# Graph kernel, two layers: source indices loaded first, and the first eight row gathers issued ahead of the branch on edge order

## Chip, cores, metric
One core of a Trainium2 chip. The metric is the device time of one execution in microseconds (us); the kernel before takes 2122.07 us, the median of three runs (2119.05, 2122.07 and 2122.08).

## What is computed
There are 6250 nodes with 128 features and 106250 edges (831 tiles of 128 edges, the last one partly filled), sorted by target node `dst` in the inputs given.

```
h = relu(layernorm(x));  x = x + segment_sum((h @ W.T + b)[src] * edge_weight, dst)        # layer 0
h = relu(layernorm(x));  m = relu([h[src], h[dst]] @ W1[t] + b1[t]) @ W2[t] + b2[t]        # layer 1, t = edge type
gi = segment_sum(m, dst) @ W_ih.T + b_ih;  gh = h @ W_hh.T + b_hh;  x = x + GRU(gi, gh, h)
```

## The kernel before
Every engine runs a straight list of instructions; semaphores tie the lists together. All engines first run a prologue, then `choose`: it waits for a flag that VectorE computes from `dst` and `edge_weight` (`dve_scan`, `dve_flag`: are the targets in an order the fast path can take, and no weight negative), loads the flag into a register and branches. With the inputs given the fast branch is taken: `f0_*` for layer 0, `f1_*` for layer 1. The other branch (`l0_*`, `l1_*`, with `sp_x`) is never run here.

In the prologue the SyncE queue loads the four edge arrays whole, 104 partitions of 1024 edges, in the order `dst`, `src`, `edge_weight`, `edge_type` (`load_edges`, three DMAs each; the second waits for a memset of VectorE, `dve_pads`). Each array is then turned so that a tile's 128 edges lie down the partitions. For `src` that is: ScalarE makes floats (L457, `act_float`), TensorE transposes eight blocks (L545, `pe_edges`), ScalarE copies them to `src_t` (L473, `act_edges`), which raises the semaphore `preC` to 1.

GpSimd issues all gathers: one indirect DMA fetches the 128 source rows (512 B each) of one tile. In layer 0 eight tiles make an octet; `f0_pool` (L1297) goes over 104 octets with a ring of `R0` = 6 buffers (`slot0`), so an octet waits for TensorE to have used the one six octets earlier (`out0`). Octets 0 to 6 gather rows of the input `x`, which are normalised after they come in (`edge_stats`, `weigh_early`). From octet 7 (`EARLY`) on the rows come from `h0_tab`, a table of normalised rows that is made meanwhile: SyncE loads `x` (L381), VectorE takes statistics, ScalarE normalises (L1469), SyncE stores (L1609), and GpSimd waits for the stores (`tab`). Ten tiles of layer 0 are fetched row by row by SyncE instead (L1647), so GpSimd issues 821 gathers. Layer 1 (`f1_pool`, L1673) starts when all of `p_tab` is stored and issues 824 more, in groups of four with a ring of ten.

VectorE's work after the flag: L634 to L644 are seven passes over 104x1024 elements (`dve_rel`, `dve_keys`), then the branch and layer 0's masks (L1312 to L1314).

Of the kernel before, what the change touches and what calls it, by code (L numbers as in the profile page):

```python
# [32 lines left out]
GT = 4  # L33
PR = 2
GP = GT // PR
NG = 4
# [8 lines left out]
def gnn_program(nc, x, src, dst, etype, eweight, W0, b0, W1, b1, W2, b2, Wih, Whh, bih, bhh, out):  # L45
    N, D = x.shape
# [4 lines left out]
    NTILE = -(-E // P)  # L51
# [3 lines left out]
    PB = NT // PR // NBLK  # L55
# [10 lines left out]
    h0_tab = nc.dram_tensor("h0_tab", [N, D], F32).ap()  # L66
# [10 lines left out]
    with ExitStack() as ctx:  # L77
        def sb(name, shape, dt=F32):
            return ctx.enter_context(nc.sbuf_tensor(name, shape, dt))
# [16 lines left out]
        dst_i, src_i, typ_i = tmp(0, I32), tmp(1, I32), tmp(2, I32)  # L96
# [6 lines left out]
        src_t = sb("src_t", [P, NCOL], I32)  # L103
# [32 lines left out]
        rowno = sb("rowno", [P, 2, UT], I32)  # L136
# [46 lines left out]
        R0, R1 = 6, 10  # L183
        FW = D + T + 1
        HR = 4
        TO = NBLK * PR
        NPAIR = NCH // 2
        NOCT = NT // (NBLK * PR)
# [6 lines left out]
        def slot0(k):  # L195
            return accs[:, F0 + k * TO * FW:F0 + (k + 1) * TO * FW].rearrange("p (t f) -> p t f", f=FW)
# [11 lines left out]
        EARLY = 7  # L208
# [5 lines left out]
        alone0, alone1 = ({k: j for j, (k, _) in enumerate(a)} for a in (ALONE0, ALONE1))  # L214
# [80 lines left out]
        s_g0 = [[sem(f"s_gather0_{q}_{h}") for h in range(2)] for q in range(R0)]  # L295
# [45 lines left out]
        LR = 96  # L341
# [11 lines left out]
        def load_edges(eng, ap, to, pads, ev):  # L353
            flat = to.rearrange("p g e -> p (g e)")
            eng.dma_start(flat[0:LR, :], ap[0:LR * OCT].rearrange("(p e) -> p e", e=OCT)).then_inc(s[ev], 16)
            eng.wait_ge(s["pads"], pads)
            eng.dma_start(flat[LR:n_full, :], ap[LR * OCT:n_full * OCT].rearrange("(p e) -> p e", e=OCT)).then_inc(s[ev], 16)
            eng.dma_start(flat[n_full:PB, 0:n_tail], ap[E - n_tail:E].rearrange("(a e) -> a e", a=1)).then_inc(s[ev], 16)
# [7 lines left out]
        W12_IN = 4 * 16  # L366

        def sp_prologue(eng):
            load_edges(eng, dst, dst_i, 1, "dst_in")
            load_edges(eng, src, src_i, 2, "src_in")  # L370
            load_edges(eng, eweight, w_a, 4, "w_in")
            load_edges(eng, etype, typ_i, 3, "typ_in")
            eng.wait_ge(s["qpad"], 1)
            eng.dma_start(q_tab[N:NPAD, :], zrows[0:NPAD - N, :]).then_inc(s["st_q"], 16)
            for k in ("st_c", "st_h", "st_p", "upd_st"):
                eng.sem_inc(s[k], 16)
# [34 lines left out]
            return v  # L411

        def sp_x(eng):
            for i, (a, b) in enumerate(PIECES):
                for h in HALVES:
                    eng.dma_start(x_rows[h, a:b, :], x_lin[h, a:b, :]).then_inc(s_x[i], 16)
            eng.wait_ge(s["xs_pad"], 1)
            for a, b in PIECES:
                for h in HALVES:
                    eng.dma_start(xs[h, a:b, 0:D], x_mod[h, a:b, :]).then_inc(s["x_again"], 16)  # L420
# [144 lines left out]
        def pool_sums(eng):  # L565
            eng.memset(xs[:, :, :], 0.0).then_inc(s["xs_pad"], 1)
# [6 lines left out]
            eng.wait_ge(s["step"], in_order[0])  # L573

        def dve_pads(eng):
            eng.memset(dst_i[LR:PB, :, :], int(FAR)).then_inc(s["pads"], 1)
            eng.memset(src_i[LR:PB, :, :], 0).then_inc(s["pads"], 1)
            eng.memset(typ_i[LR:PB, :, :], 0).then_inc(s["pads"], 1)
            eng.memset(w_a[LR:PB, :, :], 0.0).then_inc(s["pads"], 1)

# [260 lines left out]
        def l0_pool(eng):  # L841
            def sweep_end(w):

                eng.wait_ge(s["out0"], (w + 1) * (NB * NG) + RING)
                apart(eng)
                for k in (q[0] for q in s_g0[:NG]):
                    eng.dma_reset(range(k.num, k.num + 1))
                    eng.sem_clear(k)
                eng.sem_inc(s["swept0"], 1)

            h0_stored(eng)
            eng.memset(accs[:, 0:A0], 0.0).then_inc(s["zero"], 1)

            def step(j, n, q, w, left):
                g = Group(j, n, q)
                eng.wait_ge(s["idx0"], g.gi + 1)
                apart(eng)
                for t in range(GT):
                    k = g.slot * GT + t
                    eng.indirect_dma_start(G[:, g.slot, t, :], None, h0_tab,  # L860
                                           bass.IndirectOffsetOnAxis(rowno[:, 0, k:k + 1], 0)).then_inc(s_g0[g.slot][0], 16)
            layer(eng, step, lambda c, pairs, k: None, sweep_end=sweep_end)

        def l0_dve(eng):
# [95 lines left out]
        def l0_pe(eng):  # L960
            eng.sem_inc(s["out0"], RING)
            MP.start(eng)
            eng.wait_ge(s["preC"], 6)
            eng.wait_ge(s["sets"], 1)
            eng.wait_ge(s["w12_in"], W12_IN)

            def step(j, n, q, w, left):
                g = Group(j, n, q)
                eng.wait_ge(*grp("hot0", g))
                eng.wait_ge(s_g0[g.slot][0], g.gathered)  # L970
                pairs_in(eng, "acc0", g, back=1)
                o = pb[g.two]
                for t in range(GT):
                    p = t // PR
                    eng.matmul(o[:, p * WIN:(p + 1) * WIN], G[:, g.slot, t, :], nodew[:, g.slot, t, :],
                               start=t % PR == 0, stop=t % PR == PR - 1)
                for t in range(GT):
                    p = t // PR
                    ins = eng.matmul(o[0:T + 1, 256 + p * WIN:256 + (p + 1) * WIN], typew[:, g.slot, t, :],
                                     nodehot[:, g.slot, t, :], start=t % PR == 0, stop=t % PR == PR - 1)  # L980
                ins.then_inc(s["out0"], 1)

            def sweep_end(w):
                eng.wait_ge(s["swept0"], w + 1)

            def chunk(c, pairs, k):
                if k == 0:
                    MA.wait(eng, "cnt", c)
                    MD.wait(eng, "x1", c, 1)
                    MP.done(eng.transpose(pb[6][0:CW, 0:D], st[:, 0, 0:CW], ident[:, :]))  # L990
                if k == 2:
                    MD.wait(eng, "h", c)
                    MA.wait(eng, "hT", c, 1)
                    MP.done(eng.transpose(pb[6][:, 256:256 + CW], st[0:CW, 0, P:2 * P], ident[0:CW, 0:CW]))
                if k == 3:
                    MA.wait(eng, "hT", c)
                    MA.wait(eng, "p", c, 1)
                    MP.done(eng.matmul(pb[7][0:CW, :], h1s[:, :], w1a[:, :, :].rearrange("f t g -> f (t g)"),
                                       start=True, stop=True))
                    MD.wait(eng, "q", c, 1)  # L1000
                    MP.done(eng.matmul(pb[5][0:CW, :], h1s[:, :], w1b[:, :, :].rearrange("f t g -> f (t g)"),
                                       start=True, stop=True))
            layer(eng, step, chunk, sweep_end=sweep_end)
# [278 lines left out]
        def pair_at(o, after):  # L1282
            c, r = divmod(o - after - 2 * (LAG + 1), 4)
            return c if r == 0 and 0 <= c < NPAIR else None

        def f0_pool(eng):
            eng.wait_ge(s["preC"], 1)
            for o in range(NOCT):
                if o >= R0:
                    eng.wait_ge(s["out0"], o - R0 + 1)  # L1290
                if o == EARLY:
                    eng.wait_ge(s["tab"], 32 * len(T_PIECES))
                for t in range(TO):
                    k = o * TO + t
                    if k in alone0 or k >= NTILE:
                        continue
                    eng.indirect_dma_start(slot0(o % R0)[:, t, 0:D], None, x if o < EARLY else h0_tab,  # L1297
                                           bass.IndirectOffsetOnAxis(src_t[:, k:k + 1], 0)).then_inc(s_g0[o % R0][t // GT], 16)

        def f0_dve(eng):  # L1300
            eng.wait_ge(s["preC"], 4)
# [628 lines left out]
        def choose(eng, fast, general):  # L1930

            eng.wait_ge(s["prep"], 1)
            ordered = nc.values_load(flag_i[0:1, 0:1], engines=[eng.engine], min_val=0, max_val=1)
            before = in_order[0]
            with eng.If(ordered):
                for f in fast:
                    f(eng)
            in_order[0] = before
            with eng.Else():
                for f in general:  # L1940
                    f(eng)
# [44 lines left out]
        @block.gpsimd  # L1986
        def _(eng):
            pool_prologue(eng)
            pool_sums(eng)
            choose(eng, [f0_pool, f1_pool], [pool_h0, l0_pool, l1_pool])  # L1990

# [18 lines left out]
```

## Time and profile before
| | |
|---|---|
| profiled execution: time, span | 2122.12 us, 2120.3 us |
| runs | 2119.05, 2122.07, 2122.08 us |
| GpSimd (POOL) busy | 1565.8 us, 74% |
| TensorE, VectorE, ScalarE busy | 1265.0, 900.6, 571.0 us |
| DMA | 214.40 MB, mean 101 GB/s |

Span is first to last instruction of the profiled execution; its time is 1.8 us longer. GpSimd's busy share looks moderate, but it counts only the gathers themselves and not the issue gap ahead of each; the waits and the chain of work tell whether it ever stands idle for another engine.

### The profile page before, as it was taken

What the parts mean: (1) busy time and instruction counts of PE and PEld (TensorE: products, weight loads), DVE (VectorE), ACT (ScalarE), POOL (GpSimd) and SP (SyncE); (2) the same over time, 40 slices, a digit from 0 to 9 for tenths busy, and PEclk for the clock granted to TensorE, in tenths of its full rate; (3) what the DMA queues carried; (4) which work ended last, traced back from release to release, by engine and by line L of the source; (5) the groups of instructions that cost most, each with busy time, mean ns of one, the idle gap of its engine ahead of it and who ended that gap; (6) DMA issues with size and microseconds to landing.
All of it is one profiled execution on the core that took longest, in us unless ns stands there. A gap on an engine that the chain in (4) does not pass through costs nothing.

```text
span 2120.3 us, 29576 instructions
## 1 busy us (share of the span) xinstructions
PE 1265.0 (60%) x6646; PEld 1082.7 (51%) x6646; DVE 900.6 (42%) x2542; ACT 571.0 (27%) x1502; POOL 1565.8 (74%) x1658
## 2 busy tenths in 40 slices
PE   2445445445445445445556777776677667677776
PEld 2433333334334334334345676666666666666665
DVE  7633232332332333233234555555555455555454
ACT  4633333333333333333231111111111111111111
POOL 6777777777777777777567777777777777777774
PEclk7566667666666666666668877888988887888887
DMA  8323323333333333323244444444444444444442
GB/s 190 95 81 89 90 78 93 87 80 90 87 81 90 89 80 91 88 80 94 67 132 110 109 109 115 116 109 111 118 110 114 115 110 116 114 111 114 114 114 61
DMA packets 179672, 214.40 MB, mean 101 GB/s; under 512 B 55311, under 2 KB 125585, under 8 KB 178992
## 3 DMA queue, kind: packets, MB, share of 16 engines
q0 software_dynamic: 52640, 107.91, 21.0%
q1 hardware_dynamic: 125608, 103.77, 16.9%
q10 hardware_dynamic: 1244, 0.79, 0.2%
q8 instruction: 56, 0.92, 0.2%
q14 instruction: 124, 1.02, 0.2%
HBM read 176.31 MB, written 35.99 MB: 100 GB/s over the span
## 4 chain that ended last, share of the span: by engine, by line
POOL 73%; issue 24%; PE 1%; DMA 1%; DVE 1%; ACT 0%; POOLq 0%; SPq 0%; DVEq 0%; ACTq 0%
POOL accs L1297 36%; POOL G L1673 15%; POOL edge L1673 15%; POOL g_more L1673 7%; DMA accs<-in_edge_weight_dram 0%; PE bank L1580 0%; DMA accs<-h_tab,src_t 0%; PE bank L1543 0%; PE bank L1883 0%; DMA p_tab<-hot 0%; DMA edge<-p_tab,src_t 0%; ACT accs L1458 0%; PE bank L1896 0%; PE bank L1906 0%; PE bank L1907 0%
## 5 line engine op out<-in xcount | busy, mean ns | idle before, releaser
L1297 POOL DMA_INDIRECT accs<-h_tab,src_t x765 | 722.2, 944 | 233.2 <-issue 232.6
L1872 PE MATMUL bank<-qwin,hotT 128*128 128x128 f32 x1662 | 300.1, 336 | 307.7 <-DVE hotT L1760 296.9
L1543 PE MATMUL bank<-accs 128*125 128x133 f32 x1662 | 329.3, 369 | 220.8 <-ACT accs L1458 172.5
L1543 PEld LDWEIGHTS bank<-accs 128*125 128x125 f32 x1662 | 308.5, 272 | 263.4 <-issue 127.8
L1872 PEld LDWEIGHTS bank<-qwin,hotT 128*128 128x128 f32 x1662 | 255.3, 235 | 343.0 <-DVE hotT L1760 329.5
L1673 POOL DMA_INDIRECT G<-p_tab,src_t x334 | 316.1, 946 | 122.2 <-issue 101.5
L1673 POOL DMA_INDIRECT edge<-p_tab,src_t x331 | 313.8, 948 | 100.9 <-issue 100.6
L1458 ACT ACTIVATE accs<-accs,edge 128x128 f32<-128x128 f32 x765 | 244.4, 391 | 478.9 <-DMA accs<-h_tab,src_t 478.8
L1830 ACT ACTIVATE rows<-rows 128x512 f32<-128x512 f32 x208 | 130.9, 630 | 654.5 <-DVE rows L1770 637.1
L1883 PE MATMUL bank<-hot,rows 128*128 128x128 f32 x1662 | 284.8, 329 | 1.9 <-ACT rows L1830 1.1
L1883 PEld LDWEIGHTS bank<-hot,rows 128*128 128x128 f32 x1662 | 269.2, 246 | 2.3 <-ACT rows L1830 2.3
L1312 DVE COPY accs<-edge 128x8 f32<-128x8 f32 x104 | 20.1, 193 | 474.7 <-PE bank L1543 474.4
L1673 POOL DMA_INDIRECT g_more<-p_tab,src_t x159 | 151.8, 955 | 48.5 <-issue 48.5
L1580 PE MATMUL bank<-w1a,h1b 128*125 128x512 f32 x100 | 93.2, 1086 | 123.1 <-ACT h1b L1492 123.1
L1755 DVE TENSOR_TENSOR hot<-bank,key_t 128x512 f32<-128x512 f32 x208 | 141.6, 681 | 3.6 <-DMA q_tab<-hot 3.6
L1770 DVE TENSOR_TENSOR rows<-bank,G 128x512 f32<-128x512 f32 (+1 forms) x84 | 57.8, 689 | 192.5 <-DMA G<-p_tab,src_t 187.2
L1770 DVE TENSOR_TENSOR rows<-bank,edge 128x512 f32<-128x512 f32 (+1 forms) x84 | 57.4, 684 | 184.1 <-DMA edge<-p_tab,src_t 178.0
L1808 DVE TENSOR_TENSOR accs<-bank,accs 128x128 f32 x416 | 119.5, 287 | 30.6 <-DVE accs L1808 0.7
L1314 DVE TENSOR_TENSOR accs<-bank,edge 128x1000 f32<-128x1000 f32 x104 | 123.8, 1190 | 0.0
L1580 PEld LDWEIGHTS bank<-w1a,h1b 128*125 128x125 f32 x100 | 28.9, 320 | 156.4 <-ACT h1b L1492 125.0
L1558 PE MATMUL bank<-w0t,G 128*125 128x128 f32 x100 | 29.9, 452 | 120.6 <-ACT G L1476 120.6
L1896 PE MATMUL bank<-accs,w 128*128 128x125 f32 x400 | 97.9, 401 | 0.6 <-ACT st L1843 0.6
(178 smaller groups left out, 1322.1 us busy)
## 6 DMA issues: line engine op xcount, KB each, us to landing
qwin<-q_tab SPq DMA_DIRECT2D x416, 64.0 KB
hotT<-h_tab SPq DMA_DIRECT2D x1162, 0.5 KB
nodew<-key_tab SPq DMA_DIRECT2D x52, 256.0 KB
nodehot<-key_tab SPq DMA_DIRECT2D x52, 256.0 KB
w1a<-p_tab SPq DMA_DIRECT2D x778, 0.5 KB
accs<-h_tab,src_t POOLq DMA_INDIRECT x765, 2.5
p_tab<-st SPq DMA_DIRECT2D x25, 224.0 KB
p_tab<-hot SPq DMA_DIRECT2D x25, 224.0 KB
```

Source lines behind the costliest of these rows:

```text
L1297: eng.indirect_dma_start(slot0(o % R0)[:, t, 0:D], None, x if o < EARLY else h0_tab, bass.IndirectOffsetOnAxis(src_t[:, k:k + 1], 0)).then ...
L1314: eng.tensor_tensor(ones_of(o % HR), mid(iota_p[:, 0:CW], TO), bcast(rel_t[:, cols], CW), ALU.is_equal).then_inc(s["hot0"], 1)
L1458: ins = eng.activation(G0[:, t, 0:D], row, ACT.Copy, scale=w_t[:, o * TO + t:o * TO + t + 1])
L1543: ins = eng.matmul(pb[SUM_BANK[o % 4]][0:CW, 0:FW], ones_of(o % HR)[:, t, :], slot0(o % R0)[:, t, :], start=t == 0, stop=t == last)
L1580: ins = eng.matmul(pb[PQ_BANK[k]][0:CW, :], h1_pair[:, k * CW:(k + 1) * CW], weights[:, :, :].rearrange("f t g -> f (t g)"), start=True, s ...
L1673: eng.indirect_dma_start(slot1(g % R1)[:, t, :], None, p_rows, bass.IndirectOffsetOnAxis(src4_t[:, k:k + 1], 0)).then_inc(s_g1[g % R1], 16)
L1755: eng.tensor_tensor(hot[:, g % NG], mid(iota_p, GT), bcast(key_t[:, g * GT:(g + 1) * GT], KEYS), ALU.is_equal)
L1770: ins = eng.tensor_tensor(rows[:, g % 2, 0:n], got[:, 0:n], slot1(g % R1)[:, 0:n], ALU.add)
L1808: eng.tensor_tensor(a, pb[4 + g % 2][:, p * KEYS:(p + 1) * KEYS], a, ALU.add).then_inc(s["acc1"], 1)
L1830: eng.activation(rows[:, g % 2], rows[:, g % 2], ACT.Relu).then_inc(s["relu1"], 1)
L1872: ins = eng.matmul(pb[2 + g % 2][:, t * D:(t + 1) * D], hotT[:, g % HT, t * P:(t + 1) * P], qwin[:, g % NG, t // PR, :], start=True, stop= ...
L1883: ins = eng.matmul(pb[4 + g % 2][:, p * KEYS:(p + 1) * KEYS], rows[:, g % 2, t, :], hot[:, g % NG, t, :], start=t % PR == 0, stop=t % PR = ...
```

## The change
The load order becomes `src`, `dst`, `edge_weight`, `edge_type`, and VectorE's first two memsets swap with it. The body of the gather loop becomes `octet_rows`; `pool_first_octet`, which waits for `preC` and issues octet 0's eight gathers from `x`, runs on GpSimd ahead of `choose`. `f0_pool` starts at octet 1. The other lines (`sp_x`, the shift of `s_g0` by one slot) belong to the branch that isn't run: there the eight gathers have to be waited for and their semaphores kept apart.

```
         def sp_prologue(eng):
-            load_edges(eng, dst, dst_i, 1, "dst_in")
-            load_edges(eng, src, src_i, 2, "src_in")
+            load_edges(eng, src, src_i, 1, "src_in")
+            load_edges(eng, dst, dst_i, 2, "dst_in")
...
         def dve_pads(eng):
+            eng.memset(src_i[LR:PB, :, :], 0).then_inc(s["pads"], 1)
             eng.memset(dst_i[LR:PB, :, :], int(FAR)).then_inc(s["pads"], 1)
-            eng.memset(src_i[LR:PB, :, :], 0).then_inc(s["pads"], 1)
...
+        def octet_rows(eng, o, table):
+            for t in range(TO):
+                k = o * TO + t
+                if k in alone0 or k >= NTILE:
+                    continue
+                eng.indirect_dma_start(slot0(o % R0)[:, t, 0:D], None, table,
+                                       bass.IndirectOffsetOnAxis(src_t[:, k:k + 1], 0)).then_inc(s_g0[o % R0][t // GT], 16)
+
+        def pool_first_octet(eng):
+            eng.wait_ge(s["preC"], 1)
+            octet_rows(eng, 0, x)
+
         def f0_pool(eng):
-            eng.wait_ge(s["preC"], 1)
-            for o in range(NOCT):
+            for o in range(1, NOCT):
                 if o >= R0:
                     eng.wait_ge(s["out0"], o - R0 + 1)
                 if o == EARLY:
                     eng.wait_ge(s["tab"], 32 * len(T_PIECES))
...
+                octet_rows(eng, o, x if o < EARLY else h0_tab)
...
             pool_sums(eng)
+            pool_first_octet(eng)
             choose(eng, [f0_pool, f1_pool], [pool_h0, l0_pool, l1_pool])
```

GpSimd's instructions from its last memset of the prologue (`xs`) on, before: the load of the flag and the branch, then all layer 0 gathers.

```order
L566 MEMSET xs 128x6783
L1933 TENSOR_LOAD flag_i
L1933 ISA x2
L1935 COMPARE_AND_BRANCH
L1297 DMA accs<-in_x_dram,src_t 128x128 x56
L1297 DMA accs<-h_tab,src_t 128x128 x765
```

The same place on GpSimd after the change:

```order
L568 MEMSET xs 128x6783
L1293 DMA accs<-in_x_dram,src_t 128x128 x8
L1941 TENSOR_LOAD flag_i
L1941 ISA x2
L1943 COMPARE_AND_BRANCH
L1293 DMA accs<-in_x_dram,src_t 128x128 x48
L1293 DMA accs<-h_tab,src_t 128x128 x765
```

Eight of the 56 gathers from `x` now stand ahead of the load of the flag; the number of gathers is the same.

The SyncE queue's first DMAs of the program, before (`accs` holds all four edge arrays at this stage):

```order
L355 DMA accs<-in_dst_dram 96x1024
L357 DMA accs<-in_dst_dram 7x1024
L358 DMA accs<-in_dst_dram 1x778
L355 DMA accs<-in_src_dram 96x1024
L357 DMA accs<-in_src_dram 7x1024
L358 DMA accs<-in_src_dram 1x778
```

and after:

```order
L355 DMA accs<-in_src_dram 96x1024
L357 DMA accs<-in_src_dram 7x1024
L358 DMA accs<-in_src_dram 1x778
L355 DMA accs<-in_dst_dram 96x1024
L357 DMA accs<-in_dst_dram 7x1024
L358 DMA accs<-in_dst_dram 1x778
```

Two loads of the same size change places; the weights and types behind them keep theirs.

## Rows read from the trace of the kernel before
**Rows 1.** The page's chain of work that ended last.
```profile
POOL 73%; issue 24%; PE 1%; DMA 1%; DVE 1%; ACT 0%; POOLq 0%; SPq 0%; DVEq 0%; ACTq 0%
```
**Rows 2.** Waits of GpSimd: waited for: us in total, times, longest us.
```profile
POOL accs L1297 <- issue: 260.5, 819, 11.1
POOL G L1673 <- DMA p_tab<-hot: 20.6, 1, 20.6
POOL accs L1297 <- PE bank L1543: 0.6, 2, 0.3
```
**Rows 3.** Timeline of GpSimd's gathers: start, us, instruction, [idle before <-releaser].
```profile
19.08 1.14 POOL L1297 DMA_INDIRECT accs<-in_x_dram,src_t  x1 [11.11 <-issue]
20.53 1.52 POOL L1297 DMA_INDIRECT accs<-in_x_dram,src_t  x1 [0.30 <-issue]
...
23.61 0.94 POOL L1297 DMA_INDIRECT accs<-in_x_dram,src_t  x1 [0.30 <-issue]
24.86 1.98 POOL L1297 DMA_INDIRECT accs<-in_x_dram,src_t  x1 [0.31 <-issue]
27.14 0.95 POOL L1297 DMA_INDIRECT accs<-in_x_dram,src_t  x1 [0.30 <-issue]
...
30.89 0.94 POOL L1297 DMA_INDIRECT accs<-in_x_dram,src_t  x1 [0.30 <-issue]
...
90.80 0.94 POOL L1297 DMA_INDIRECT accs<-h_tab,src_t  x1 [0.30 <-issue]
```
**Rows 4.** Timeline of VectorE and ScalarE up to the flag.
```profile
7.29 1.24 DVE L585 TENSOR_SCALAR accs<-accs 104x1024 f32<-104x1024 int32 x1 [2.06 <-DMA accs<-in_dst_dram]
11.04 1.06 ACT L457 ACTIVATE accs<-accs 104x1024 f32<-104x1024 int32 x1 [5.33 <-DMA accs<-in_src_dram]
11.76 0.15 DVE L600 TENSOR_TENSOR top<-top,base_f 104x4 f32<-104x4 f32 x1
13.90 1.66 ACT L473 ACTIVATE src_t<-bank 128x416 int32<-128x416 f32 x2 [1.80 <-PE bank L545]
14.43 1.22 DVE L602 TENSOR_REDUCE late<-accs 104x4 f32<-104x1024 f32 x1 [2.51 <-DMA accs<-in_edge_weight_dram]
17.20 0.14 DVE L617 CAST flag_i<-badp 1x1 int32<-1x1 f32 x1
```
**Rows 5.** Chain of work across GpSimd's branch (POOLq is its sequencer).
```profile
17.62 0.26 POOLq L1933
...
18.21 0.87 issue
```
**Rows 6.** Chain of work where layer 1's gathers start.
```profile
1065.77 0.04 POOLq L1665
1065.82 0.72 issue
```
**Rows 7.** Timeline of VectorE beside the first gathers.
```profile
18.44 0.74 DVE L634 TENSOR_SCALAR accs<-accs,oct_f 104x1024 f32<-104x1024 int32 x1
19.22 0.76 DVE L635 TENSOR_SCALAR accs<-accs,oct_f 104x1024 f32<-104x1024 f32 x1
20.01 1.22 DVE L636 TENSOR_TENSOR accs<-accs 104x1024 f32<-104x1024 f32 x1
...
23.66 1.23 DVE L643 SCALAR_TENSOR_TENSOR accs<-accs 104x1024 f32<-104x1024 f32 x1
24.80 1.22 DVE L644 SCALAR_TENSOR_TENSOR accs<-accs 104x1024 bf16<-104x1024 f32 x1
...
26.79 1.19 DVE L1314 TENSOR_TENSOR accs<-bank,edge 128x1000 f32<-128x1000 f32 x1
```
**Rows 8.** Timeline and waits of SyncE's queue at the last table store.
```profile
75.84 2.26 SPq L1635 DMA_DIRECT2D hotT<-in_src_dram  x2
...
SPq L1635 <- DMA h_tab<-nodew: 1.8, 1, 1.8
```
**Rows 9.** Timeline of TensorE's sums of octets 0 and 2.
```profile
49.25 3.88 PE L1543 MATMUL bank<-accs 128*125 128x133 f32 x16 [21.63 <-ACT accs L1442]
...
72.08 3.88 PE L1543 MATMUL bank<-accs 128*125 128x133 f32 x16 [6.17 <-ACT accs L1442]
```

More of the change, by code:

```diff
@@ L413, in sp_x @@
         def sp_x(eng):
+            for h in range(2):
+                eng.wait_ge(s_g0[0][h], 16 * GT)
             for i, (a, b) in enumerate(PIECES):
@@ L845, in sweep_end @@
                 apart(eng)
-                for k in (q[0] for q in s_g0[:NG]):
+                for k in (q[0] for q in s_g0[1:NG + 1]):
                     eng.dma_reset(range(k.num, k.num + 1))
@@ L860, in step @@
                     eng.indirect_dma_start(G[:, g.slot, t, :], None, h0_tab,
-                                           bass.IndirectOffsetOnAxis(rowno[:, 0, k:k + 1], 0)).then_inc(s_g0[g.slot][0], 16)
+                                           bass.IndirectOffsetOnAxis(rowno[:, 0, k:k + 1], 0)).then_inc(s_g0[g.slot + 1][0], 16)
             layer(eng, step, lambda c, pairs, k: None, sweep_end=sweep_end)
@@ L969, in step @@
                 eng.wait_ge(*grp("hot0", g))
-                eng.wait_ge(s_g0[g.slot][0], g.gathered)
+                eng.wait_ge(s_g0[g.slot + 1][0], g.gathered)
                 pairs_in(eng, "acc0", g, back=1)
@@ L1292, in f0_pool @@
                     eng.wait_ge(s["tab"], 32 * len(T_PIECES))
[L1293 to L1298, printed above, removed]
+                octet_rows(eng, o, x if o < EARLY else h0_tab)
         def f0_dve(eng):
```

## The prediction, made before the changed kernel ran
> **What bounds the kernel now.** I read the chain of work that ended last first: 73% of it is GpSimd and 24% "issue" [rows 1]. The reader is to see that no other engine has more than 1%. GpSimd's waits come next, since "issue" may hide anything. Its longest idle times are 11.1 us ahead of the first gather and 20.6 us between the layers; other engines' releases sum to 0.6 us in layer 0 [rows 2]. That 0.6 us is two gaps of 0.3, the usual gap, so it is no wait either. Then the gathers' timeline: each takes 0.94 us and the next starts 0.30 us after it. From the gather at 30.89 to the one at 90.80 there are 48, so the pace is 59.91 / 48 = 1.248 us [rows 3]. So from 19.08 us to the end of layer 0, and again in layer 1, the kernel is one unbroken stream of gathers. The 20.6 us in the middle follow from the last gather of layer 0 (its rows, their sums, the last chunk, its store), and so does the tail behind the last gather of layer 1. Whatever the stream starts earlier, the end comes earlier by, unless a gather meets a wait that it did not meet before.
>
> What decides the start is two things together: `src_t` has to be there (ScalarE's copies end at 13.90 + 1.66 = 15.56 us [rows 4]) and the flag (17.34 us [rows 4]) with the branch behind it. The flag came last: it waited for the weights at 14.43 us [rows 4].
>
> **The change, step by step.** All times are in the profiled execution (2122.12 us, span 2120.3), which agrees with the median of the runs (2122.07) to 0.05 us.
>
> Step 1, `src` loaded first. The first array of the queue is in at 7.29 us, the second at 11.04 us [rows 4]; both loads are of one size, so they trade places. `src` comes 3.75 us earlier. ScalarE is free then: it had been idle for 5.33 us before 11.04 [rows 4], so since 5.71. The way from there to `preC` is unchanged, 15.56 - 11.04 = 4.52 us, so `preC` comes at 11.81 us.
>
> Step 2, the first gather. GpSimd's memset ends at 19.08 - 11.11 = 7.97 us [rows 3], so it stands ready. What lies between a released semaphore and a gather's start is shown where layer 1 begins: 0.04 + 0.72 us [rows 6]. First gather at 12.57 us, against 19.08: 6.5 us earlier.
>
> Step 3, eight gathers and then the branch. Eight at the undisturbed pace are 9.98 us. The flag is late now: VectorE gets `dst` at 11.04, its passes up to L600 took 11.91 - 7.29 = 4.62 us [rows 4] and end at 15.66, so L602, which started at 14.43, starts at about 15.72. All VectorE's work behind it moves by 1.29 us, the flag to 18.63. That is behind the weights no longer but still 3.9 us before GpSimd's eighth gather is done (12.57 + 9.98 = 22.55), so the flag costs GpSimd nothing; if the gathers didn't cover it, it would cost the 1.29 us. The branch costs: from the load of the flag to the first gather 17.62 to 19.08 = 1.46 us [rows 5], of which 0.30 is the gap that any gather has: 1.16 us. Its lower bound is 0.87 - 0.30 = 0.57 us, if the load overlaps the running gather; its upper one is 19.08 - 17.34 - 0.30 = 1.44 us. I take 1.16, since the load has to wait for its turn in the same list. The ninth gather would start at 22.55 + 1.16 = 23.71 us instead of 30.89: 7.18 us, less what VectorE takes away.
>
> Step 4, what VectorE takes. Before, the first eight gathers took 11.81 us, 1.83 more than 9.98: they are 1.14, 1.52 and 1.98 us long where 0.94 is usual [rows 3]. The gather at 20.53 starts within L636 (20.01 to 21.23), the one at 24.86 within L644 (24.80 to 26.02); the lengthening, 0.58 and 1.04 us, is the rest of those passes less 0.12 us. The gather at 23.61 starts 0.05 us before L643 and is not lengthened, nor is the one at 27.14, well inside L1314, which reads PSUM and one SBUF array [rows 3, 7]. So a gather that starts while a pass over two SBUF arrays (or one of the 0.74 us passes, L634, L635) runs waits for its end. After the change these passes lie 1.29 us later: L634 from 19.73, L636 from 21.30, the last, L644, from 26.09 to 27.31. The gathers that start among them: the seventh, at 12.57 + 7.49 = 20.06, in L634 (+0.3); the eighth, at 21.6, in L636, which ends at 22.52 (+0.8); the ninth at 24.8 and the tenth at 26.05, where L643 ends and L644 begins, a matter of 0.05 us whether it costs nothing or 1.1. So 1.1 to 2.3 us, with 0 as the lower bound (no gather hits) and some 3.5 as the upper one (each hit costs near a full pass). I take 1.7, the middle, close to the 1.83 of before.
>
> The Trainium skill, "SBUF — State Buffer", section "Who interferes with whom", says that VectorE instructions with at most one SBUF input outside the two-port modes don't contend with GpSimd. Here L586, L590 and L602, reductions of 1.2 us over one SBUF array, come to lie beside the first three gathers, which the trace of before doesn't show. By the rule they cost nothing and the sum stays; if they held gathers up as L636 does, the gain would be about 4.8 us by the same reckoning, or 3.7 with L644 on top.
>
> Step 5, what the other engines lose. Everything behind the flag on SyncE, ScalarE and VectorE starts 1.29 us later. That is hidden by the stream if tables and ring keep ahead of it. The ring: octet 6 starts at 80.82 (90.80 less eight paces) and needs octet 0's sums, done at 53.13; octet 8 at 100.78 needs octet 2's, done at 75.96 [rows 3, 9]. 25 us of room, of which at most 9 go. The table: its last store is seen landed at 77.6 (75.84 + 1.8 [rows 8]) and is wanted at 90.80 less the gain, about 85.3. Even 1.29 us later it leaves 6 us.
>
> **Sum:** 6.5 + 1.83 - 1.16 - 1.7 = 5.5 us less; 2122.1 - 5.5 = **2116.6 us** (-0.26%). The likeliest case's own range is a gain of 4.3 to 7.2 us, 2114.9 to 2117.8.
>
> **Rivals.**
> (A) More gain: no gather is held up and the branch overlaps: 7.18 + 0.59 = 7.8 us, 2114.3 us. For it speaks that hits depend on fractions of a microsecond; against it that VectorE's two-input passes follow each other without gaps for 7 us just then.
> (B) VectorE gives back more: the one-input passes count, or the tenth gather waits out L644, with up to 3.5 us in all: gain 3.7 us or less, 2118.4 us, the same within what can be told. Against it: the gather within L1314 took 0.95 us.
> (C) The table decides: octet 7's first gather waits for `h_tab`. From a landing at 84.5 us on it eats the gain, and beyond 90.0 us the kernel is slower; it would have to come over 12 us later than 77.6. Eight gathers (512 KB) now run beside the loads of weights and types, and ScalarE's normalising passes are a chain of in-order work that starts 1.29 us later, so a few us are thinkable. Should they grow to 17 us (the table landing at 94.6), the price is 94.6 + 0.76 - 90.80 = 4.6 us: 2126.7 us. But octet 0's rows arrive earlier than before, and VectorE had waited for them, which pulls the same chain forward.
> (D) The start moves and the end doesn't, because another engine sets the pace later: no change, 2122 us. The waits of GpSimd speak against it: nothing but its own pace in both layers.
>
> **Chances.** Forecast 0.68; A 0.07; B 0.15; C 0.04, nearly all slower; D 0.06. 0.2% of 2122 us is 4.2 us, about what a measurement can tell from no change. Forecast and A are faster by more (0.75), B and D lie within (0.21), C is slower (0.04). The range goes from A to a little beyond B, 2114.2 to 2119.0; outside it are C, D and the rest of B.
>
> **What the changed kernel's profile would show.** The first gather at 12.6 us; the ninth at 24.8 to 26 behind a gap of about 1.5 us; ScalarE's first L457 pass at 7.3 and VectorE's first pass at 11.0; `flag_i` at about 18.5. Octet 7's first gather at about 85.3 with a gap of 0.30 ahead of it: a longer gap there is rival C. Layer 1's first gather at about 1061.0 against 1066.53, with the same 20.6 us ahead of it. I am wrong if the first gather costs GpSimd something once that was hidden before the flag, if `src` lands later than 7.3, or if the flag comes after 22.5 us.

## The result, and the profile after
The changed kernel takes **2113.6 us** (median of 6 runs, 2111.39 to 2115.55), the kernel before 2121.56 us in 6 runs on the same chip. The ratio is 0.9964, with a 95% interval of 0.9952 to 0.9977: 7.6 us faster (4.9 to 10.2). The forecast was 2116.6 us with a range from 2114.2 to 2119.0, so the sign was right and the time came out 0.6 us below the low end. Three of the six runs of after lie at 2111.4 to 2112.1 us and three at 2115.1 to 2115.6; the median is a number between them.

The profiled execution of after took 2115.55 us (span 2113.8), 6.6 us less than that of before. Its chain of work that ended last, and the waits of GpSimd (waited for: us in total, times, longest us):

```profile
POOL 73%; issue 24%; PE 1%; DMA 1%; ACT 0%; DVE 0%; POOLq 0%; SPq 0%; DVEq 0%; ACTq 0%
```
```profile
POOL accs L1293 <- issue: 248.8, 816, 0.3
...
POOL G L1681 <- DMA p_tab<-hot: 21.2, 1, 21.2
POOL accs L1293 <- ACT src_t L475: 3.7, 1, 3.7
POOL accs L1293 <- PE bank L1551: 0.6, 2, 0.3
```

The bound is the same stream of gathers as in [rows 1, 2]. The 11.1 us that looked like "issue" are gone: GpSimd now waits 3.7 us for `src_t`, and no gap of layer 0 behind that is longer than 0.3 us. The timeline of GpSimd's gathers after (answers to [rows 3]):

```profile
11.66 1.22 POOL L1293 DMA_INDIRECT accs<-in_x_dram,src_t  x1 [3.68 <-ACT src_t L475]
13.18 0.94 POOL L1293 DMA_INDIRECT accs<-in_x_dram,src_t  x1 [0.30 <-issue]
...
20.67 1.10 POOL L1293 DMA_INDIRECT accs<-in_x_dram,src_t  x1 [0.30 <-issue]
22.07 0.96 POOL L1293 DMA_INDIRECT accs<-in_x_dram,src_t  x1 [0.30 <-issue]
...
25.85 1.97 POOL L1293 DMA_INDIRECT accs<-in_x_dram,src_t  x1 [0.31 <-issue]
28.12 0.94 POOL L1293 DMA_INDIRECT accs<-in_x_dram,src_t  x1 [0.30 <-issue]
...
83.05 0.94 POOL L1293 DMA_INDIRECT accs<-h_tab,src_t  x1 [0.30 <-issue]
```

The ninth gather, the first behind the branch, is the one at 22.07. The gap ahead of it is 0.30 us like any other: the branch cost nothing. ScalarE and VectorE up to the flag and beside the gathers (answers to [rows 4, 7]):

```profile
6.86 1.06 ACT L459 ACTIVATE accs<-accs 104x1024 f32<-104x1024 int32 x1 [1.15 <-DMA accs<-in_src_dram]
9.71 1.66 ACT L475 ACTIVATE src_t<-bank 128x416 int32<-128x416 f32 x2 [1.80 <-PE bank L547]
11.18 0.69 DVE L587 TENSOR_SCALAR accs<-accs 104x1024 f32<-104x1024 int32 x1 [5.95 <-DMA accs<-in_dst_dram]
...
13.24 1.22 DVE L592 TENSOR_REDUCE top<-accs 104x4 f32<-104x1024 f32 x1
15.42 1.22 DVE L604 TENSOR_REDUCE late<-accs 104x4 f32<-104x1024 f32 x1
18.18 0.14 DVE L619 CAST flag_i<-badp 1x1 int32<-1x1 f32 x1
...
20.20 0.76 DVE L637 TENSOR_SCALAR accs<-accs,oct_f 104x1024 f32<-104x1024 f32 x1
25.79 1.22 DVE L646 SCALAR_TENSOR_TENSOR accs<-accs 104x1024 bf16<-104x1024 f32 x1
```

And the chain of work across the branch (answers to [rows 5]):

```profile
18.18 0.68 POOL accs L1293
...
18.88 0.17 POOLq L1941
...
19.09 0.03 POOLq L1941
...
19.15 0.04 POOLq L1943
19.19 0.23 issue
19.42 0.94 POOL accs L1293
```

The sixth gather runs from 18.18 to 19.12. In that time GpSimd's sequencer finishes the load of the flag (L1941); it has branched (L1943) by 19.19 us. Two more gathers that stand ahead of the branch in the list, at 19.42 and 20.67, have not started then. So the sequencer was past all eight when only six had begun.

### The profile page after: what moved, and what is told of

It is laid out like the page before. It is cut to its first block, busy times and chain, and to the rows that moved or that the text cites. A ratio compares the mean times of both kernels' runs of the same rounds, so it can differ in the third digit from the quotient of the medians.

```text
span 2113.8 us, 29576 instructions
## 1 busy us (share of the span) xinstructions
PE 1258.0 (60%) x6646; PEld 1074.7 (51%) x6646; DVE 900.6 (43%) x2542; ACT 570.2 (27%) x1502; POOL 1565.7 (74%) x1658
## 4 chain that ended last, share of the span: by engine, by line
POOL 73%; issue 24%; PE 1%; DMA 1%; ACT 0%; DVE 0%; POOLq 0%; SPq 0%; DVEq 0%; ACTq 0%
POOL accs L1293 36%; POOL G L1681 15%; POOL edge L1681 15%; POOL g_more L1681 7%; PE bank L1588 0%; DMA accs<-h_tab,src_t 0%; PE bank L1551 0%; DMA accs<-in_src_dram 0%; DMA p_tab<-hot 0%; DMA edge<-p_tab,src_t 0%; ACT accs L1466 0%; PE bank L1904 0%; PE bank L1914 0%; PE bank L1915 0%; ACT src_t L475 0%
## 5 line engine op out<-in xcount | busy, mean ns | idle before, releaser
L1880 PE MATMUL bank<-qwin,hotT 128*128 128x128 f32 x1662 | 293.5, 331 | 311.3 <-DVE hotT L1768 299.7
L1880 PEld LDWEIGHTS bank<-qwin,hotT 128*128 128x128 f32 x1662 | 248.8, 229 | 347.5 <-DVE hotT L1768 332.5
```

Of the source, the lines that this page charges most:

```text
L1880: ins = eng.matmul(pb[2 + g % 2][:, t * D:(t + 1) * D], hotT[:, g % HT, t * P:(t + 1) * P], qwin[:, g % NG, t // PR, :], start=True, stop= ...
```

## Experiments
Two kinds of chip turned up. The first result and E8 to E11 come from chips on which the kernel before takes about 2121 us; on the chips of E0 to E7 it takes about 2737 us. There the gathers have the same pace, but the small instructions of the other lists come late from some 110 us on: the row loads of SyncE follow each other every 1.65 us in E0 and every 0.47 us in after, and GpSimd waits for its neighbours all through both layers. The groups of these loads in the timeline of SyncE's queue, of E0 (cut off at 130 us) and then of after (xcount is their number; all 38 take 70.51 us in E0):

```profile
111.25 16.46 SPq L1655 DMA_DIRECT2D hotT<-h_tab  x10
```
```profile
80.35 18.04 SPq L1655 DMA_DIRECT2D hotT<-h_tab  x38
```

So from E0 to E7 I use the profile of the first 30 us, and the times only for what they bound, some 0.25%. Where the time mattered the same kernel went to the other chip again: E0, E7 and E10 are the changed kernel itself, E11 is E1 again, E8 is E2 and E9 is E6.

**Order alone, early gathers alone, both (E0, E1, E2; E7; E8, E10, E11).** E1 swaps the loads and memsets and leaves all gathers behind the branch:

```
         def sp_prologue(eng):
-            load_edges(eng, dst, dst_i, 1, "dst_in")
-            load_edges(eng, src, src_i, 2, "src_in")
+            load_edges(eng, src, src_i, 1, "src_in")
+            load_edges(eng, dst, dst_i, 2, "dst_in")
```

E2 is the changed kernel with this swap undone: eight gathers ahead of the branch, `dst` first.

> The changed kernel once more, for a second profile and more times. The runs of it so far lie in two groups (2111.4 to 2112.1 and 2115.1 to 2115.6 us) and the profile was taken from one of 2115.6. If the groups differ in the pace of the gathers, a profile from the lower group shows layer 1's first gather near 1059.7 and a shorter layer 1 or layer 0; if they differ at the start, the first gather differs from 11.66 us. I expect the start to be alike to 0.1 us and 2111 to 2116 us.

> Only the load order and the memsets swapped; all gathers stay behind the branch. Theory (the start is set by the later of indices and flag, and only the eight early gathers can use the indices): the flag comes 0.98 us later, as it did after the change (18.32 against 17.34), so the first gather at 20.06 us and the time 1.0 us more than before, 2122.6. Rival (earlier indices are worth something by themselves, through ScalarE's or TensorE's chains): faster than before by 1 us or more.

> Only the eight early gathers, with the targets loaded first as before. Theory (the branch is hidden behind gathers that are already handed over): indices ready at 15.56 us as before, first gather at 15.9, the ninth with the usual gap of 0.30 us; 3.2 us gained at the start and 1.83 less some 1.5 of lengthened gathers, so 3.5 us faster than before, 2118.0. Rival (the branch costs its 1.16 us behind the eighth gather): 2.4 us faster, and a gap of 1.46 us ahead of the ninth.

> The changed kernel once more beside the three below. The last four runs were on a chip where the kernel before took 2736 us instead of 2122, SyncE's row loads setting the pace. If this chip is like the first one, 7 to 8 us faster than before (2113 to 2115); if it is like the second, no difference that can be told, and only the first 40 us of each profile can be compared. Either way the first gather at 11.4 to 11.7 us and the ninth behind the usual gap of 0.30 us.

On the second chip the ratios to before are 0.9985 (0.996 to 1.0011) for E0, 0.9964 (0.9936 to 0.9992) for E7, 0.9997 (0.9972 to 1.0021) for E1 and 0.9974 (0.9949 to 0.9999) for E2. They overlap and order nothing. The two groups that E0 was to tell apart can't be seen on that chip. The start of the stream was plain: first gather at 11.60 us in E0 and 11.50 in E7, 19.40 in E1, 15.34 in E2. On the first kind of chip:

> Only the eight early gathers, targets loaded first, timed again: on the second chip the profile gave a first gather at 15.34 us and the ninth at 27.67, 3.2 us ahead of the kernel before. If the chip is like the first one (before at 2122 us), 3.2 us faster than before, within 1 us (2118.3). If it is like the second, nothing that can be told in three rounds.

> The changed kernel beside the other three, as the one to compare them with. On a chip like the first one 2113.6 us and 7.6 us faster than before; on one like the second, 2731 against 2737 as the first 24 runs of it there gave on average.

> Only the load order, timed again: on the second chip its first gather stood at 19.40 us against 19.08 in the kernel before. On a chip like the first one 0.3 to 1.0 us slower than before, 2122.2.

| | time, us | ratio to before (2120.71) | first gather | 9th gather |
|---|---|---|---|---|
| E11 order alone | 2122.32 | 1.001 (1.0 to 1.0019) | 20.18 | 31.99 |
| E8 early alone | 2117.8 | 0.9987 (0.9977 to 0.9996) | 15.81 | 28.30 |
| E10 both | 2113.25 | 0.9963 (0.995 to 0.9975) | 11.60 | 22.98 |

GpSimd's first gather in E11, and in E8 the first and the ninth:

```profile
20.18 1.14 POOL L1297 DMA_INDIRECT accs<-in_x_dram,src_t  x1 [12.20 <-issue]
```
```profile
15.81 1.14 POOL L1293 DMA_INDIRECT accs<-in_x_dram,src_t  x1 [7.83 <-ACT src_t L475]
...
28.30 0.94 POOL L1293 DMA_INDIRECT accs<-in_x_dram,src_t  x1 [0.30 <-issue]
```

Order alone makes the first gather 1.10 us later than [rows 3], since the flag is later, and costs 1.6 us (at the edge of what the runs tell). The early gathers alone start 3.3 us sooner and win 2.9 us. Both together win 7.5 us, not 1.3: while the flag comes last, earlier indices are worth nothing; once the gathers wait for the indices, an earlier index is an earlier gather (15.81 us in E8, 11.60 in E10). E10 repeats the first result in other runs.

**How long the cover has to be (E3, E4).** E3 issues 16 gathers ahead of the branch, E4 only four:

```
+            octet_rows(eng, 1, x)                        # E3, behind octet_rows(eng, 0, x)
-            octet_rows(eng, 0, x)
+            octet_rows(eng, 0, x, range(GT))             # E4: GT is 4; the rest follow in f0_pool
```

> As after the change, but sixteen gathers (octets 0 and 1) ahead of the branch. Theory (the branch is hidden already with eight): the same time as after the change, within 1 us. If GpSimd's sequencer runs far ahead of the gathers, it loads the flag at 18.9 us as before; if it is only two or three gathers ahead, it gets there not before 27 us and the time is the same all the same. Rival (something of the branch is still on the path): 0.5 to 1.2 us faster.

> As after the change, but only four gathers ahead of the branch. Theory (what hides flag and branch is the length of the early gathers): the fourth ends near 16.6 us, the flag comes at 18.3, so the fifth starts at 19.4 us, where the seventh stood before, 2.5 us later than after the change; 2.0 to 2.7 us slower than the changed kernel. Rival (the flag is never waited for, only the load and jump cost): at most 1.2 us slower, with the fifth gather near 17 to 18 us.

GpSimd's fourth and fifth gather in E4:

```profile
15.57 0.94 POOL L1292 DMA_INDIRECT accs<-in_x_dram,src_t  x1 [0.30 <-issue]
19.52 1.16 POOL L1292 DMA_INDIRECT accs<-in_x_dram,src_t  x1 [3.01 <-DVE base_i L624]
```

With four ahead the stream runs dry before the flag is there and stands still for 3.01 us, 2.7 more than the usual gap. With eight it never does, and 16 gain nothing more: the twelfth gather starts at 27.46 us in E3 and at 27.65 in E0. In the times both are inconclusive, 0.9979 (0.995 to 1.0008) for E3 and 0.9988 (0.9967 to 1.0008) for E4: the hole is shown in the profile, its price in the time is not. How far the sequencer runs ahead, E3 shows too. The instructions that touch the flag, by tile (min/median/max ns, first and last start):

```profile
L620 DVE CAST flag_i<-badp x1: 141/141/141, 17.5 to 17.5; 1x1 int32<-1x1 f32 x1
...
L1943 POOLq TENSOR_LOAD <-flag_i x1: 490/490/490, 17.7 to 17.7; - x1
```

GpSimd's sequencer starts the load at 17.7 us, as soon as the flag is written. By then five of the 16 gathers ahead of it in the list have started (11.41 to 16.59 us; the sixth starts at 17.84). So the sequencer was past eleven that had not begun.

**The room of the table (E5).** `EARLY` = 6 asks for `h_tab` one octet sooner.

```
-        EARLY = 7
+        EARLY = 6
```

> As after the change, but the gathers read the table from octet 6 on instead of 7. Prices the room of the table: its last store landed at 77.5 us and octet 6's first gather was at 73.1 after the change. Theory (the stream is one chain, so any wait of a gather shows in full): a gap of about 5 us ahead of octet 6 and the time 4.5 us more than the changed kernel, so that a table 6 us late in the changed kernel would cost nothing and each us beyond its full price. Rival (the ring or the rest of layer 0 takes the wait in): less than 2 us more.

On that chip the table is late anyway: GpSimd waits 20.60 us for it ahead of octet 7 in E0, and 36.47 us ahead of octet 6 in E5, where some 5 us were expected. The ratio, 1.0013 (0.9981 to 1.0044), settles nothing for the chip of the prediction. There the profile of after has the answer. SyncE's last store of the table, and the row behind it:

```profile
74.92 0.77 SPq L1617 DMA_DIRECT2D h_tab<-nodew  x2
75.72 2.26 SPq L1643 DMA_DIRECT2D hotT<-in_src_dram  x2
```

The second row starts 0.12 us before its like in [rows 8], so the stores are no later than they were, and octet 7's first gather at 83.05 has a gap of 0.30 us. What a late table costs on that chip was not measured.

**Earlier still (E6, E9).** If the start of the indices is what counts, 16 tiles' worth of them can come by a way of their own: a small load of `src[0:2048]` ahead of all others, one cast, one transpose, one cast back to `few_t`, and 16 gathers from it ahead of the branch. GpSimd's memset of `xs` (5.74 us) goes to ScalarE, and `EARLY` becomes 8.

```
         def sp_prologue(eng):
+            eng.dma_start(few_i[:, :], src[0:16 * P].rearrange("(k e) -> k e", e=P)).then_inc(s["upd_ld"], 16)
...
-            eng.memset(xs[:, :, :], 0.0).then_inc(s["xs_pad"], 1)
...
-            eng.wait_ge(s["preC"], 1)
-            octet_rows(eng, 0, x)
+            eng.wait_ge(s["shift"], 1)
+            octet_rows(eng, 0, x, few_t)
+            octet_rows(eng, 1, x, few_t)
```

The wait for `preC` goes behind the branch, to the start of `f0_pool`. The kernel uses four semaphores of the branch that isn't run; that branch would have to be renumbered.

> Further than the change: the 2048 source indices of octets 0 and 1 come by a load of their own ahead of the edge arrays, are cast by VectorE and turned by TensorE; sixteen gathers run ahead of the branch, ScalarE instead of GpSimd zeroes the sums (6783 columns), and the table is read from octet 8 on. Theory (only the start of the stream counts): first gather at 5.8 us instead of 11.66, no wait ahead of the seventeenth, 5 to 6 us faster than the changed kernel (2107.5 to 2109). Rival (gathers beside the edge loads delay flag and table, and VectorE's passes hold up more gathers): 2 us faster or less.

> The early 2048 source indices with sixteen gathers ahead, timed again: its first gather stood at 6.08 us and its twentieth at 32.40, where the changed kernel's twentieth stood at 37.6, so 5.2 us ahead. On a chip like the first one 5 us faster than the changed kernel, 2108.5, unless a wait for the table comes ahead of octet 8 (it was 3.0 us on the second chip, where all other engines are slower).

E6: 0.9972 (0.9946 to 0.9998) on the second chip. E9: **2109.03 us** (4 runs), ratio 0.9938 (0.9922 to 0.9955), 11.7 us faster than before and 4.2 faster than the changed kernel on the same chip (E10), where 5 were expected; the intervals of the two against before just overlap. GpSimd's first gather:

```profile
6.08 1.14 POOL L1306 DMA_INDIRECT accs<-in_x_dram,g_more  x1 [3.79 <-DVE g_more L594]
```

That is 5.6 us before after's, of which 4.6 are left at the 21st gather (33.48 us against 38.12); against E10 it is 5.5 us at both places (11.60 and 39.01). By its median it is the fastest version found.

## Why the prediction was right, and where it fell short
**The bound and the sign: right.** Nothing but its own pace holds GpSimd in either layer, and an earlier start comes out at the end almost whole. Rival D fell. Rival C fell too: the table was in time with some 5 us to spare (75.72 + 1.8 us against 83.05), where step 5 had 6 us.

**Steps 1 and 2: the mechanism right, sizes off by 0.91 us.** The first gather came at 11.66, not 12.57. Half of it, 0.43 us, is the landing of the first array: its pass starts at 6.86 where I took 7.29, a spread between executions and chips (6.25 us in E2 and 7.20 in E8, which are one kernel; 7.25 in E11, 6.79 in E10). The rest is the way from the released semaphore to the gather. I took 0.76 us from [rows 6]; the trace of after has 11.38 to 11.66, 0.28 us, and so has E8 (15.53 to 15.81). At the start of layer 1 it is 0.72 us behind the sequencer's own instruction in after as in before; why the two places differ is not shown.

**Step 3, the flag: right; the branch: wrong, and this is the step that failed.** The flag was ready at 18.32 us (0.98 later than before, forecast 1.29), early enough. But I charged 1.16 us for the branch, with a lower bound of 0.57, "since the load has to wait for its turn in the same list". My bounds both came from a branch in front of which GpSimd stood idle; they could not show what a branch costs behind queued work. Of rival A's two conditions the overlap came true, and more fully than it had it; the other, that no gather is held up, did not. Its 7.8 us against the 7.76 measured below are luck.

**Step 4: the mechanism right, the size partly luck.** After's first twelve gathers take 28.12 - 11.66 - 12 x 1.248 = 1.48 us more than their pace (forecast 1.7). Of that 0.20 us is the first gather itself, a term that the forecast didn't name: it lasts 1.14 us in the profiles of before and of E0 to E11. So VectorE took about 1.3 us. The rule read from [rows 3, 7] held: the gather at 20.67 lies in L637 and lasts 0.16 us longer, the one at 25.85 starts 0.06 us into L646 and waits out the pass (1.03 us), and the first, 1.22 us here, starts in L587 (11.18 to 11.87), a pass that step 4 didn't count. But these are not the gathers that I had named. In E0, E7 and E10, the same kernel, the flag came 0.4 to 0.5 us sooner, and the seventh, eighth and eleventh gather were hit. E10's rows:

```profile
11.60 1.14 POOL L1293 DMA_INDIRECT accs<-in_x_dram,src_t  x1 [3.62 <-ACT src_t L475]
...
19.28 1.44 POOL L1293 DMA_INDIRECT accs<-in_x_dram,src_t  x1 [0.30 <-issue]
...
21.02 1.65 POOL L1293 DMA_INDIRECT accs<-in_x_dram,src_t  x1 [0.30 <-issue]
...
25.49 1.98 POOL L1293 DMA_INDIRECT accs<-in_x_dram,src_t  x1 [0.30 <-issue]
27.77 0.94 POOL L1293 DMA_INDIRECT accs<-in_x_dram,src_t  x1 [0.30 <-issue]
```

By the same reckoning E10 lost 27.77 - 11.60 - 11 x 1.248 = 2.44 us, E0 2.32 and E7 2.39. So after's 1.48 is the low one of four, and VectorE's share is 1.3 to 2.2 us, within the 1.1 to 2.3 of step 4. The rule itself is rough: in E10 the gather at 19.28 has 0.53 us of L636 (19.07 to 19.81) ahead of it and lasts 0.50 us longer, not 0.41, and in E9 one that starts at 12.52, ahead of L600 (12.75), lasts 0.09 us longer. The gather that starts at 15.68 in after, within L604 (15.42 to 16.64), a reduction over one SBUF array, lasts 0.94 us. In E10 the gathers at 13.04 and 15.54 start within L592 (12.94 to 14.16) and L604 (14.99 to 16.21) and last 0.94 us as well. By the rule of the Trainium skill, "SBUF — State Buffer", section "Who interferes with whom", they should not contend; the trace agrees, and the first form of rival B fell. In its second form a gather did wait out the last pass (the twelfth in after, the eleventh in E0, E7 and E10), which the range of step 4 held.

**The sum.** At the 13th gather (28.12 us, against 30.89 + 4 x 1.248 = 35.88) the stream led by 7.76 us where I had 5.5. The difference is 0.91 + 1.16 + 0.22 (step 4) = 2.29 us: the three terms close it. They close E10's lead as well, 35.88 - 29.02 = 6.86 us: 5.5 + 0.97 (start) + 1.16 (branch) - 0.74 (gathers held up) = 6.89. Of the lead 7.75 us are left at octet 7 (83.05 against 90.80), 6.83 us at the first gather of layer 1 (1059.70 against 1066.53) and 6.92 at the last gather. The wait between the layers was 21.21 us in after and 20.65 in before, but 21.23 to 21.43 in E8, E10 and E11, of which E11 has all gathers behind the branch like before: the profiled execution of before had a short one, and that 0.6 us is none of the change's.

**The tail, which the forecast took as fixed.** The branch alone doesn't put the time outside the range: the lead of 6.92 us at the last gather, taken off 2122.1 us, gives 2115.2, and the profiled execution of after took 2115.55, both inside it. The rest lies behind the last gather. I had let the tail follow the stream unchanged; it has a length of its own, 18.3 to 22.4 us in the six profiles of this kind of chip. The windows from the last gather to the end, of before, after, E8, E11 and E10 (stretch, us, busy us and count of PE, PEld, DVE, ACT, POOL, then granted clock, DMA share, GB/s):

```profile
2098.30:2120.30 22.00, 12.97 (x56) 10.93 (x54) 8.98 (x30) 4.14 (x11) 0.91 (x1) 0.57 0.08 20
```
```profile
2091.40:2113.80 22.40, 12.94 (x56) 10.90 (x54) 8.97 (x30) 4.13 (x11) 0.90 (x1) 0.57 0.08 20
```
```profile
2095.90:2117.20 21.30, 12.00 (x56) 10.07 (x54) 8.89 (x30) 4.13 (x11) 0.94 (x1) 0.76 0.08 20
```
```profile
2099.70:2118.60 18.90, 10.26 (x56) 8.33 (x54) 8.98 (x30) 4.13 (x11) 0.94 (x1) 0.83 0.09 24
```
```profile
2091.40:2109.70 18.30, 8.89 (x56) 7.07 (x54) 8.88 (x30) 4.13 (x11) 0.92 (x1) 0.91 0.09 24
```

The same 56 matmuls take 12.94 us in after at a mean granted clock of 0.57 and 8.89 us in E10 at 0.91, and the tail is 4.1 us longer; E8 and E11 lie between. The means mix the two levels: after has 1.00 (2.4 GHz) up to 2094.5 us and 0.50 (1.2 GHz) from 2095.0 on, E10 has 1.00 up to 2106.5. From 2092 to 2094 us TensorE is busy for 1.04 us in after and 1.07 in E10, so what lets the clock fall in one of them is not shown. After and E10 issue their last gather at 2091.35 and 2091.38 us and end 4.1 us apart, as far as after's two groups of runs are. That the tail is what parts the groups is likely but not shown, since the other runs have no trace; E10's six runs fill part of the space between (2112.51, 2114.00).

So the lead in the profiles (6.5 to 7.8 us) and the difference of the medians (7.5 to 8) are the same within 1.5 us, and closer they can't be brought.

## What to carry to other kernels
Where one engine's stream sets the time from start to end, four places count: what it waits for first, its gaps, the gaps between stages and the tail, which can be 4 us longer in one execution than in the next. List every prerequisite of the first item; here the indices and the flag both had to move, and one of them alone gave 2.9 us or cost 1.6, where both gave 7.5. To hide a decision, put work that doesn't depend on it ahead of it in the same list, long enough to last until the decision is ready: four gathers left a hole of 2.7 us, eight none, 16 no gain more. And take the price of a branch or a wait from a place where the engine has work queued, if that is where it will stand.

## What the runs showed of the hardware
- GpSimd's sequencer was past eleven indirect DMAs that had not begun (E3), and the load of a flag and a branch behind queued ones cost 0 us where they cost 1.16 us in front of an idle engine [rows 5]. The Trainium skill, "Advanced Engine Details and Errata", section "Engine Queue Depths", gives GpSimd a depth of 8. For these gathers the trace has eleven, and the measurement decides.
- A pass of VectorE over 104x1024 elements, integer to float, takes 0.69 us in after and 1.24 us in before [rows 4], where it starts at 7.29 while GpSimd's memset runs until 7.97. The extra 0.55 us is the rest of the memset less 0.13: the same pattern as with the gathers, the other way round. E8, with `dst` first again, has 1.33 us from 7.20 on, and E2 2.29 us from 6.25 on: all three end at 8.53 or 8.54 us. That the memset is the cause wasn't tested by itself.
- The mean of a gather can differ a little between executions: its median is 944 ns in before, after and E10, and 947 ns in the profiled execution of E9, which at 1645 gathers would be 5 us. It was also the slowest of E9's four runs (2113.96 us; the others 2106.38 to 2109.43). The groups of layer 1's gathers by line, before and E9 (min/median/max ns):

```profile
L1673 POOL DMA_INDIRECT G<-p_tab,src_t x334: 940/944/1207, 1066.5 to 2080.7; - x167
```
```profile
L1696 POOL DMA_INDIRECT G<-p_tab,src_t x334: 942/947/1167, 1056.8 to 2074.0; - x167
```

- The chips differ: 2121 us on one kind, 2737 us on another for the same kernel, with the gathers at the same pace (mean 944 ns in after, 946 in E0) and SyncE's row loads 1.65 us apart where they are 0.47 apart. Why is not shown.
